# A block-diagonal mask made by GpSimd in four pieces instead of by VectorE in one

## The reference, cut to what matters

```
def ffn(x, Wq, Wk, Wv, Ws, Wd, Wo):          # H=16 heads, DH=64, E=8 experts, K=2
    q, k  = einsum('btc,hdc->bhtd', x, Wq), einsum('btc,hdc->bhtd', x, Wk)
    gate_v = einsum('btc,hec->bthe', x, Ws)
    w, sel = top_k(gate_v, K)
    mix_v  = sum over k of sigmoid(w) * one_hot(sel, E)
    v      = einsum('bthe,bted->bhtd', mix_v, einsum('btc,edc->bted', x, Wv))
    attn   = softmax(q * DH**-0.5 @ k.T) @ v                       # bihd
    _, sel_o = top_k(einsum('btc,hec->bthe', x, Wd), K)
    mask_o = one_hot(sel_o, E).sum(axis=3)                         # 0 or 1
    return einsum('bthe,bthd,efd->bthf', mask_o, attn, Wo).sum(axis=2)
```

## Time and profile before

| | us |
|---|---|
| median of 3 runs (lowest, highest) | 551.34 (551.05, 553.38) |
| the profiled execution, whole | 552.02 |
| its span, first to last instruction | 550.0 |
| DVE busy | 468.2 (85%) |
| PE busy | 437.6 (80%) |
| ACT busy | 293.3 (53%) |
| POOL busy | 143.1 (26%), all in the first 225 us |

### The profile page before, as it was taken

The page is one execution under the profiler, slowest core; times in us unless marked ns, Lnnn a source line. Parts: engine busy times, 40 slices in busy tenths (PEclk is TensorE's granted clock), DMA queues, the critical chain, the costliest instruction groups (busy, mean ns, idle before and its releaser), DMA issues.

```text
span 550.0 us, 25189 instructions
## 1 busy us (share of the span) xinstructions
PE 437.6 (80%) x10768; PEld 366.0 (67%) x10768; DVE 468.2 (85%) x850; ACT 293.3 (53%) x400; POOL 143.1 (26%) x125
## 2 busy tenths in 40 slices
PE   1466889889988998658887888788888888887864
PEld 0245777777777877547776776677676767676754
DVE  2987778887888895579999999999999999999962
ACT  1254756766675674425544554555555455545631
POOL 8262767775777685000000000000000000000000
PEclk9987999999999999678999999999999999999996
DMA  7814443454345300000000000000000000000000
GB/s 175 265 40 133 137 155 116 135 182 141 114 161 177 120 1 4 1 1 3 8 3 4 4 4 0 4 4 2 2 4 4 0 4 4 4 0 4 7 7 5
DMA packets 18124, 29.44 MB, mean 54 GB/s; under 512 B 2988, under 2 KB 13996, under 8 KB 18092
## 3 DMA queue, kind: packets, MB, share of 16 engines
q1 hardware_dynamic: 18092, 28.97, 16.9%
HBM read 28.05 MB, written 0.92 MB: 53 GB/s over the span
## 4 chain that ended last, share of the span: by engine, by line
DVE 43%; PE 33%; issue 14%; ACT 6%; DVEq 1%; DMA 1%; SPq 1%; POOL 1%; ACTq 0%; POOLq 0%
DVE ctxf_all L856 8%; PE ps L958 6%; PE ps L1201 5%; DVE ctxf_all L827 5%; DVE rs L844 3%; PE ps L989 3%; DVE ctxT L653 3%; DVE ah L874 2%; DVE attnf L866 2%; ACT ah L557 2%; PE ps L1004 2%; PE ps L1005 2%; PE ps L1006 2%; PE ps L1014 2%; PE ps L1126 1%
## 5 line engine op out<-in xcount | busy, mean ns | idle before, releaser
L369 POOL TENSOR_TENSOR nat<-ctxf_all,nat 128x640 f16<-128x640 f32 x32 | 70.6, 2223 | 50.1 <-ACT nat L442 50.1
L958 PE MATMUL ps<-ident,nat 128*128 128x128 f16 x768 | 60.9, 225 | 10.0 <-DVE ctxT L653 5.2
L442 ACT CAST nat<-ctxf_all 128x1536 f16<-128x1536 f32 x32 | 45.5, 1470 | 39.2 <-PE ps L1006 39.2
L856 DVE TENSOR_TENSOR ctxf_all<-mixp,diag_h 128x3584 f16<-128x3584 f16 x32 | 63.2, 2014 | 0.0
L958 PEld LDWEIGHTS ps<-ident,nat 128*128 128x128 f16 x768 | 46.2, 100 | 23.4 <-issue 13.0
L1098 PE MATMUL ps<-xn,mT 128*128 128x112 f16 x256 | 41.9, 218 | 11.2 <-DVE mixp L851 11.2
L375 POOL TENSOR_TENSOR p<-pf,p 128x672 f16<-128x672 f32 x32 | 46.1, 1460 | 12.8 <-ACT pf L455 12.8
L653 DVE COPY ctxT<-ps 128x1024 f16<-128x1024 f16 x64 | 42.7, 685 | 4.7 <-PE ps L958 4.7
L1201 PE MATMUL ps<-ctxf_all,ah 128*64 128x112 f16 x1024 | 29.6, 219 | 18.5 <-DVE ah L874 18.4
L447 ACT COPY ctxT<-ps 128x1024 f16<-128x1024 f16 x32 | 33.0, 1033 | 20.3 <-PE ps L958 20.3
L973 PE MATMUL ps<-qk_cur,ctxT 128*128 128x56 f16 x384 | 33.5, 188 | 12.6 <-DVE ctxT L653 10.7
(11 more groups left out here) (169 smaller groups left out, 1288.3 us busy)
## 6 DMA issues: line engine op xcount, KB each, us to landing
ctxf_all<-in_ctx_dram SPq DMA_DIRECT2D x32, 704.0 KB
ctxf_all<-in_ctx_dram SPq DMA_DIRECT2D x32, 46.0 KB
x_all<-in_x_dram SPq DMA_DIRECT2D x2, 448.0 KB
out_dram<-y_all SPq DMA_DIRECT2D x32, 28.0 KB
ctxf_all<-in_ctx_dram SPq DMA_DIRECT2D x32, 18.0 KB
fwq_nat<-in_L_ffn_Wq_dram SPq DMA_DIRECT2D x1, 512.0 KB, 9.2
fwk_nat<-in_L_ffn_Wk_dram SPq DMA_DIRECT2D x1, 512.0 KB, 9.6
fwv_nat<-in_L_ffn_Wv_dram SPq DMA_DIRECT2D x1, 256.0 KB, 5.8
```

The source lines that it names most:

```text
L369: pool.tensor_tensor(nat[k][:, 1, 7 * C:], ctxf[k][:, 7 * C:], nat[k][:, 0, 7 * C:], ALU.subtract).then_inc(natlo2, 1)
L442: act.copy(nat[k][:, 0, :], ctxf[k][:, :]).then_inc(nathi, 1)
L856: last = dve.tensor_tensor(dv[:, part, :, :, :], mixp[:, part, :, :].unsqueeze(2).broadcast_to((P, 2 * NQ, HALF, H)), diag_h[:, :, :].unsq ...
L958: last = pe.transpose(ps[:, (3 * b + c) % 2, :].bitcast(F16)[:, P * (j % 8):P * (j % 8) + P], nat[k][:, j // TK, C * (j % TK):C * (j % TK) ...
```

## The change

The mask is no longer made by DVE in one instruction in every iteration; POOL makes it, in four instructions of 896 elements each, in a loop of its own behind its work of the first stage. Piece q waits until PE has finished the q-th group of matmuls on the old mask, for which PE now raises `f_a` after each group. PE waits for piece q before group q. The wait counts of `f_a` and `f_dm` are scaled by NQ = 4 elsewhere. POOL has an additional wait for constants (`c_dve`), which DVE writes at the start of the program.

```diff
@@ block.gpsimd, at its end
             keep(NP - 1)
 
+            def masks(i):
+
+                pool.wait_ge(c_dve, 3 + 8)
+                after(pool, f_mo, i + 1)
+                for q in range(NQ):
+                    k = slice(HG * q, HG * q + HG)
+                    after(pool, f_a, NQ * (i - 1) + q + 1 if not isinstance(i, int) or i > 0 else 0)
+                    pool.tensor_tensor(dm[:, k, :, :, :].rearrange("p k r t j -> p (k r) t j"),
+                                       chosen[:, NQ * HG + HG * q:NQ * HG + HG * q + HG, :].rearrange("p k (r j) -> p (k r) j", r=2).unsqueeze(2).broadcast_to((P, 2 * HG, HALF, E // 2)),
+                                       diag_e[:, :, :].unsqueeze(1).broadcast_to((P, 2 * HG, HALF, E // 2)), ALU.mult).then_inc(f_dm, 1)
+
+            masks(0)
+            with pool.Fori(1, NP) as i:
+                masks(i)
@@ block.scalar, iteration
-                    after(act, f_a, i - 1)
+                    after(act, f_a, NQ * (i - 1))
...
-                    after(act, f_a, i)
+                    after(act, f_a, NQ * i)
@@ block.vector, second
-                after(dve, f_dm, i)
+                after(dve, f_dm, NQ * i)
                 dve.tensor_tensor(chosen[:, :, :], oh1[:, :, :], oh2[:, :, :], ALU.add).then_inc(f_mo, 1)
@@ block.vector
-            def masks(i):
-
-                dve.wait_ge(f_mo, i + 1)
-                after(dve, f_a, i)
-                dve.tensor_tensor(dm[:, :, :, :, :].rearrange("p k r t j -> p (k r) t j"),
-                                  chosen[:, NQ * HG:, :].rearrange("p k (r j) -> p (k r) j", r=2).unsqueeze(2).broadcast_to((P, 2 * NQ * HG, HALF, E // 2)),
-                                  diag_e[:, :, :].unsqueeze(1).broadcast_to((P, 2 * NQ * HG, HALF, E // 2)), ALU.mult).then_inc(f_dm, 1)
@@ block.vector, iteration
-                    after(dve, f_a, i - 1)
+                    after(dve, f_a, NQ * (i - 1))
...
                 if nxt:
                     low_tokens(i + 1)
-                if front:
-                    masks(i)
                 if nxt:
                     top_two(i + 1)
@@ block.tensor, iteration
-                    after(pe, f_dm, i)
                     for q in range(NQ):
+                        after(pe, f_dm, NQ * (i - 1) + q + 1)
                         if q % 2 == 0:
                             after(pe, f_alo, 2 * i - 1 + q // 2)
...
-                    last.then_inc(f_a, 1)
+                        last.then_inc(f_a, 1)
```

## The result

| | before | after |
|---|---|---|
| median of 4 runs, us (lowest, highest) | 551.23 (551.05, 553.38) | 578.89 (576.93, 579.29) |
| span of the profiled execution, us | 550.0 | 577.4 |
| one iteration of the FFN loop, us | 18.73 | 20.45 or 20.60 |

The changed kernel is slower: ratio 1.0484, 95% interval 1.0464 to 1.0504. (All ratios are worked out from the single runs, not from the medians, so they differ a little from the quotient of the medians.) The mask is off DVE, and DVE's loop is still longer.

A forecast was written before the change was run, and what follows sets the result against it. DVE was taken to bound the FFN loop. 14 iterations x 2.7 us plus 2 for iteration 0 gave 39.8, so span 589.8, execution 591.8, median 591 us; own range 586 to 599, wider range 566 to 619.

The forecast's parts named there:

- the cost of a piece: POOL's 896-element mask instruction: 1.9 us, bounds 1.78 to 2.1, scaled from POOL's 672-element two-input instruction.
- What is late next: DVE behind the removed mask: the maximum of the gates waits for ACT's g_sb, so 0.74 us gained, not 1.94.
- Start of the pieces: POOL in the FFN loop: piece 0 starts at 414.35 and all four run back to back.
- DVE is held: FFN loop: DVE's two-SBUF-input instructions wait for a whole POOL piece; 2.7 us lost an iteration, the 0.74 saving included.
- the two orders: FFN loop: L779 runs before piece 2, 2.4 us later than now, or piece 2 gets in first, 3.1 later.
- rival (c): POOL's mask pieces cheaper, 1.5 us each: 573 us in all; chance 0.08.
- rival (a): PE's clock drops after longer waits for y_all: 1 to 1.8 us an iteration, 14 to 25 more, 605 to 616; chance 0.13.
- Iteration 0: First FFN iteration: mix waits 1.9 us for piece 0, later pieces delay dv; 1.1 to 2.8 us lost, 2 taken.
- The added waits: PE's waits for pieces, its added semaphores, and DVE's wait for all four pieces before chosen: all at nothing.
- (b): POOL's mask pieces dearer: 641 us with 2.86 us a piece, 619 with 2.45; chance 0.12.
- (d): FFN loop: POOL waits and DVE doesn't, chosen then waits for pieces; 0.9 us an iteration, 566 us; chance 0.06.
- (e): FFN loop: neither engine waits, faster at 540 us; decides at a DVE delay under 0.74 us an iteration; chance 0.08.

The follow-up runs named there:

- e1: Changed kernel with POOL making only the first mask and DVE none, so pairs 1 to 15 use pair 0's mask: 544.76 us, ratio 0.9861.
- e3: Changed kernel with each POOL piece replaced by a 2-element product and two memsets, as busy but only writing: 542.87 us, ratio 0.9813.
- e4: Changed kernel with the mask made in one POOL instruction of 3584 elements instead of four pieces: 598.87 us, ratio 1.0853.
- e5: Changed kernel with the mask in eight POOL pieces of 448 elements: 572.13 us, ratio 1.0344.
- e11: As e6, but POOL also makes a fifth group of heads (224 elements) in its own instruction, DVE the other 11: 545.37 us, ratio 0.9885.
- e8: Changed kernel with POOL's second operand (diag_e) in fp32, values the same: 575.94 us (two runs).
- e6: Changed kernel with POOL making piece 0 only and DVE the other 12 of 16 groups of heads: 547.84 us, ratio 0.9916.
- e12: The kernel of e6 measured again, with five rounds: 548.27 us, ratio 0.9923.
- e2: Kernel before with only the change's added PE waits and semaphores, mask still one DVE instruction: 552.59 us, ratio 0.9997.

## Why the prediction came out as it did

The direction, the mechanism and the place were right; the size was 12 us too large (591 against 578.89). The range from 566 to 619 holds the measured time, but the forecast's own range from 586 to 599 does not, nor does an iteration of 20.45 or 20.60 us lie in its 21.2 to 21.9. The step that was mis-sized is the cost of a piece. Point by point:

**What is late next.** Right: 0.74 us was worked out for the removal, e1 gives 0.76, with a wait of 1.10 us for `g_sb` in the trace.

**Start of the pieces.** 414.35 in the time of rows 3, where the scores' maximum stood at 414.14. In the changed kernel the maximum starts at 411.04 and POOL at 411.25: the same 0.21 us. Right.

**DVE is held.** Right, by two instructions (L794, L796) and for the whole of POOL's instruction; e3 and e4 show the two halves of it. It was the second of the two orders that were worked out: piece 2 gets in before L794. One premise had no row: the prediction let the reductions pass because they have one input, while its own rows have a cast and a copy with one input that were held. The premise came out right: L792, beside a piece, kept its 0.42 us, and so did L798 in e5.

**The cost of a piece.** This term was mis-sized. I took 1.9 us with bounds of 1.78 to 2.1 by scaling L375; a piece is 1.69 us, below these bounds and 11% from the 1.9 that the prediction named as the sign of being right. The lengths of 448, 896 and 3584 elements (0.936, 1.688 and 6.204 us) lie on one line: 0.18 us and 1.68 ns an element. The single group of heads in e11, 224 elements, took 0.560 us and lies on it too. L375 and L369 at their shortest, less the same 0.18, have 1.88 and 1.90 ns. I had the row of another access pattern and made its bounds too narrow; rival (c), with 1.5 us and 573, was nearer than the forecast. The Trainium skill's 2.6 cycles an element (GPSIMD Engine Reference, section 3.1), an estimated 1.94 us a piece, is not what this shape shows; the measurement decides.

A second, smaller part: a piece that had to wait for DVE holds it for less than its full length. Behind L794's end at 416.51 the last piece let L796 go at 418.21 - 0.29 = 417.92, 1.41 us later. Presumably some of the 0.18 us of fixed cost was spent while waiting; no run shows it apart.

A third: pieces that stand back to back start 1.65 us apart, not 1.69, and DVE is let go some 0.14 us before the recorded end of the piece (L794 at 416.51 - 0.42 = 416.09, 4.84 us behind the first piece's start). The cast of the first stage shows the same: it ended at 31.35, not at POOL's 31.11 plus its own 0.39.

With these the second order gives: three pieces from 414.35 to 419.19, L779's 0.42, 1.41 more, so L781 at 421.02 instead of 419.29: 1.73. The trace has 20.45 - 18.73 = 1.72 us in the iterations at the full clock, where 2.7 was forecast. This is a working behind the fact: the 4.84 and the 1.41 are read from the same trace.

The 2.7 was a middle between the two orders, 2.4 and 3.1. With 1.69 in place of 1.9 and nothing else changed, only the second order is left, and it gives 2.2 instead of 3.1. So the cost of a piece is 0.9 of the error, the two smaller parts are 0.5, and taking the middle between the orders hid 0.4 of it; that was luck. (The 3.2 for pieces of 2.1 us is a slip: the prediction's own rule, four pieces less 5.1, gives 3.3.)

**The clock, rival (a).** It is there, at less than a tenth of its price. Two neighbouring iterations of the changed kernel, cut at the scores' maximum:

```profile
411.04:431.64 20.60, 17.20 (x449) 14.44 (x445) 18.81 (x30) 9.87 (x15) 6.81 (x4) 0.92 0.01 3
431.64:452.08 20.44, 15.73 (x449) 13.14 (x445) 18.65 (x30) 9.98 (x15) 6.81 (x4) 1.00 0.01 3
```

The matmuls that follow on `y_all`, L1134 in the kernel before and L1139 in the changed one (there in both of these iterations):

```profile
421.21 1.08 PE L1134 MATMUL ps<-fwvT,xnT 128*32 128x128 f32 x32 [0.31 <-DVE y_all L893]
```
```profile
419.84 1.93 PE L1139 MATMUL ps<-fwvT,xnT 128*32 128x128 f32 x32 [2.04 <-DVE y_all L898]
...
440.44 1.08 PE L1139 MATMUL ps<-fwvT,xnT 128*32 128x128 f32 x32 [2.04 <-DVE y_all L898]
```

PE idles 2.04 us before L1139, and 0.31 before L1134. L1139 then took 1.93 us in the first of the two iterations and 1.08 in the second, so the same idle time does not always bring the lower clock. L1139 takes 1.7 to 1.94 us in five iterations of the trace, and these five are the ones of 20.60 to 20.62 us. In e8, whose pieces are as long, its like takes 1.08 us every time and no iteration between the second distance and the last is above 20.47. The cost is 0.15 us in five iterations, 0.7 us in all (the 14 distances sum to 287.5 us against 286.8 in e8), where 14 to 25 was put.

**Iteration 0.** `mix` lasted 1.81 us instead of 0.29, a wait of 1.5 us (1.9 was forecast), and the scores' maximum came 2.03 us later (246.89 against 244.86). The distance to the next maximum is no clean number: 19.47 us before and 20.62 after, but 17.92 in e8, 18.28 and 19.47 in two executions of the same kernel (e6, e12). PE's clock is only partly up there (from 236 to 256 us 0.74 on the mean before and in e6 and e8, 0.66 in e12, 0.50 in the changed kernel). The same 0.74 goes with 19.47, 18.28 and 17.92 us, so the clock alone does not explain this distance.

**The sum.** 2.03 up to the first maximum, then 1.15 in the first distance, then 24.8 for the 14 distances behind it (1.77 each), less 0.6 at the tail: 27.4 us of span, against 39.8 forecast. The 12.4 us between them are 13.0 from the delay of an iteration, 14 x (2.7 - 1.77), split as above, less 1.2 for the start (3.2 where 2 was put), plus 0.6 for the tail.

**The added waits.** At nothing, right: e2 for PE's, and no wait before `chosen` in the trace for DVE's.

**Rivals (b), (d) and (e)** are out: a piece takes 1.69 us and not 2.45 or more, and L794 does wait. But (e) named the point from which it would turn: a delay below 0.74 us. e6 and e11 are on the other side of it, since their pieces end before DVE wants the read path.

## What to carry to other kernels

An idle engine isn't free if it shares a path with the busy one. Before work is moved from VectorE to GpSimd, list VectorE's instructions in the window where it will run: here those that read PSUM and the reductions went on beside it, those with two SBUF inputs waited until the GpSimd instruction that reads SBUF was over. One input is no safe sign: a cast, a copy and a tensor-scalar in SBUF were held as well (4.69, 0.76 and 1.11 us), the tensor-scalar even beside a GpSimd memset. Move no more than fits beside the instructions that pass: here that was 1.7 to 2.2 us of it, worth 0.8 to 1.2%, while twice as much cost 1%, not half of it in the loop itself, and all of it 4.8%. And before counting a removed instruction at its length, look what the next one would wait for: here 0.76 of 1.94 us was to be had.

## What the runs showed of the hardware that was not expected

GpSimd's two-input instruction with runs of four and repeated operands is a straight line over 224 to 3584 elements, 0.18 us and 1.68 ns an element, faster than L369 and L375 (1.9 ns), with an fp32 operand as well and for a subtraction as well.

VectorE's tensor-scalar with all operands in SBUF is held as well: in iteration 0 of the changed kernel the normalisation took 1.11 us for its usual 0.34, behind POOL's second piece (237.95 to 239.69).

```profile
236.33 1.81 DVE L827 TENSOR_TENSOR mix<-sg,chosen 128x128 f32<-128x128 f32 x1
...
238.67 1.11 DVE L784 TENSOR_SCALAR xn<-x_all,mv_all,st_rstd 128x128 f32<-128x128 f32 x1
```

And here writing is enough. In e3 the same instruction met a memset that reads nothing, and took 0.81 us, while `mix`, with two SBUF inputs, took 0.31 beside the memset ahead of it:

```profile
236.92 0.85 POOL L428 MEMSET ctxf_all<- 128x896 f16 x1
...
236.20 0.31 DVE L830 TENSOR_TENSOR mix<-sg,chosen 128x128 f32<-128x128 f32 x1
...
237.03 0.81 DVE L787 TENSOR_SCALAR xn<-x_all,mv_all,st_rstd 128x128 f32<-128x128 f32 x1
```

So a GpSimd instruction that only writes lets VectorE's two-input instructions pass and not this one. It happens once in e3, in iteration 0; that it was the memset is read from the times and wasn't varied.

Executions of one kernel differ by some 5 us (e6 from 544.63 to 549.42; the kernel before from 549.28 to 555.93), and TensorE's clock at the end is the larger part of it in the two that were compared. The stretch from the last maximum to the end in two executions of the same kernel, e6 (spans 542.5) and e12 (547.6):

```profile
521.34:542.50 21.16, 11.55 (x329) 10.13 (x323) 7.96 (x12) 6.88 (x8) 1.69 (x1) 0.97 0.03 7
```
```profile
523.46:547.60 24.14, 14.47 (x329) 12.80 (x323) 7.96 (x12) 6.87 (x8) 1.69 (x1) 0.71 0.03 6
```

At a mean granted clock of 0.71 instead of 0.97 this tail takes 3.0 us longer. The other 2 us are at the start of the stage, where the clock differs too (0.74 and 0.66 from 236 to 256 us).
